# Pacing indirect stores and weight loads, and a re-ordered last stage, in a decoder layer with a mixture of experts

## The reference

```python
def _attn(q_in, k_in, v_in, wq, bq, wk, bk, wv, bv, wo, bo, causal):
    Q = (q_in @ wq + bq).reshape(Bq, Sq, H, HD)      # K, V likewise
    scores = jnp.einsum('bqhd,bkhd->bhqk', Q, Kp) / jnp.sqrt(jnp.float32(HD))
    if causal: scores = jnp.where(mask, scores, -jnp.inf)
    o = jnp.einsum('bhqk,bkhd->bqhd', jax.nn.softmax(scores, axis=-1), V)
    return o.reshape(Bq, Sq, Dm) @ wo + bo

def _moe(x, rw, rb, w1, b1, w2, b2):
    topw, topi = jax.lax.top_k(jax.nn.softmax(xf @ rw + rb, axis=-1), K)
    topw = jax.nn.softmax(topw, axis=-1)
    combine = zeros((T, E)).at[arange(T)[:, None], topi].add(topw)
    h = gelu(einsum('td,edf->etf', xf, w1) + b1[:, None, :])
    eo = einsum('etf,efd->etd', h, w2) + b2[:, None, :]
    return einsum('etd,te->td', eo, combine)

x = _layernorm(x + _attn(x, x, x, ..., True), ln1_g, ln1_b)
x = _layernorm(x + _attn(x, encoder_output, encoder_output, ..., False), ln2_g, ln2_b)
x = _layernorm(x + _moe(x, ...), ln3_g, ln3_b)
```

## Time and profile before

| | before |
|---|---|
| runs | 1040.5, 1038.59, 1041.3 us |
| the profiled execution's own time | 1039.41 us |
| its span (first to last instruction) | 1037.7 us |
| TensorE busy | 977.9 us (94%) |
| ScalarE busy | 585.7 us (56%) |
| VectorE busy | 566.6 us (55%) |
| GpSimd busy | 351.7 us (34%) |
| granted clock of TensorE | 0.9 or more in all slices but three at 0.8 |

### The profile page before, as it was taken

The page is one execution under the profiler, slowest core; times in us unless marked ns, Lnnn a source line. Parts: engine busy times, 40 slices in busy tenths (PEclk is TensorE's granted clock), DMA queues, the critical chain, the costliest instruction groups (busy, mean ns, idle before and its releaser), DMA issues.

```text
span 1037.7 us, 18756 instructions
## 1 busy us (share of the span) xinstructions
PE 977.9 (94%) x6068; PEld 583.6 (56%) x6069; DVE 566.6 (55%) x949; ACT 585.7 (56%) x1201; POOL 351.7 (34%) x481
## 2 busy tenths in 40 slices
PE   5899999999999999999998999988978999999975
PEld 3446444343445543445533354226977999999964
DVE  3646587777767777776777777804221221112127
ACT  2364556777765677765666757865323343443452
POOL 8465962343144443214445042122131111111114
PEclk9999999999999999999999999989998999999988
DMA  7623452003024012108114030022030343333143
GB/s 213 165 79 102 107 135 82 23 19 105 2 69 116 22 42 55 40 1 259 39 48 123 2 92 1 6 83 67 18 108 29 112 132 116 111 106 125 37 127 126
DMA packets 71936, 84.22 MB, mean 81 GB/s; under 512 B 10688, under 2 KB 65472, under 8 KB 71744
## 3 DMA queue, kind: packets, MB, share of 16 engines
q1 hardware_dynamic: 66368, 66.06, 22.2%
q0 software_dynamic: 5504, 17.34, 5.0%
HBM read 38.89 MB, written 12.63 MB: 50 GB/s over the span
## 4 chain that ended last, share of the span: by engine, by line
PE 86%; DMA 3%; SPq 3%; ACT 2%; issue 2%; DVE 2%; POOL 1%; another core or an unknown queue 1%; DVEq 0%; ACTq 0%; POOLq 0%
PE o_bank L798 16%; PE a_bank L781 15%; PE v_slot L1242 11%; PE v_slot L754 11%; PE a_bank L1234 9%; PE a_bank L722 6%; PE a_bank L737 3%; PE o_bank L1234 3%; PE v_slot L758 3%; PE v_slot L820 2%; SPq L498 2%; PE v_slot L806 1%; PE a_bank L702 1%; PE v_slot L759 1%
## 5 line engine op out<-in xcount | busy, mean ns | idle before, releaser
L969 DVE TENSOR_REDUCE max_q<-v_slot 128x1 f32<-128x1024 f32 (+3 forms) x352 | 399.6, 1172 | 115.0 <-PE v_slot L754 72.3
L912 ACT ACTIVATE probs<-a_bank 128x512 f32<-128x512 f32 (+1 forms) x688 | 364.2, 588 | 127.8 <-PE a_bank L781 115.9
L781 PE MATMUL a_bank<-q_stack_cross,k_stack_cross 99*128 99x512 bf16 x512 | 166.0, 386 | 7.3 <-issue 5.4
L1248 ACT ACTIVATE hidden<-a_bank,b 128x128 f32<-128x128 f32 x216 | 79.1, 368 | 163.6 <-PE a_bank L1234 141.5
L754 PE MATMUL v_slot<-k_stack_cross,q_stack_cross 96*128 96x512 bf16 x512 | 148.8, 383 | 2.5 <-DMA k_stack_cross<-parts 2.4
L798 PE MATMUL o_bank<-probs,v_cross 128*32 128x512 f32 x1024 | 133.3, 607 | 0.1
L1242 PE MATMUL v_slot<-stack_or_weights,hidden 128*128 128x256 f32 x576 | 131.0, 381 | 1.1 <-DVEq L1078 1.1
L1234 PE MATMUL a_bank<-x_col,stack_or_weights 128*128 128x128 f32 x864 | 112.6, 282 | 7.2 <-ACT hidden L1248 3.7
L1242 PEld LDWEIGHTS v_slot<-stack_or_weights,hidden 128*128 128x128 f32 x576 | 107.1, 191 | 14.7 <-DVEq L1078 1.3
L1234 PEld LDWEIGHTS a_bank<-x_col,stack_or_weights 128*128 128x128 f32 x864 | 108.5, 198 | 9.7 <-issue 4.1
L781 PEld LDWEIGHTS a_bank<-q_stack_cross,k_stack_cross 99*128 99x128 bf16 x512 | 44.9, 98 | 118.5 <-ACT probs L912 68.8
(11 more groups left out here) (210 smaller groups left out, 1162.0 us busy)
## 6 DMA issues: line engine op xcount, KB each, us to landing
stack_or_weights<-in_e_w SPq DMA_DIRECT2D x16, 1024.0 KB, 6.5
stack_or_weights<-parts SPq DMA_DIRECT2D x96, 128.0 KB, 2.4
k_stack_cross<-parts SPq DMA_DIRECT2D x96, 128.0 KB, 2.5
q_stack_cross<-parts SPq DMA_DIRECT2D x48, 128.0 KB, 2.4
inputs<-in_ctxT POOLq DMA_DIRECT2D x4, 1024.0 KB, 6.7
y_got<-token_out SPq DMA_DIRECT2D x16, 256.0 KB, 6.1
x_slots<-slots_in SPq DMA_DIRECT2D x30, 129.0 KB
inputs<-in_xT POOLq DMA_DIRECT2D x4, 512.0 KB, 6.0
```

What stands on the lines that cost most here:

```text
L781: last = nc.tensor.matmul(bank[:, i * cols:(i + 1) * cols], lhs, q_stack[kind][0:KM, G * u + j, q0:S], start=True, stop=True)
L912: nc.scalar.activation(probs[tile % PB][:, js[0]:js[-1] + 1, q0:S], a_bank[at % AS][:, 0:len(js) * (S - q0)].rearrange("p (j t) -> p j t", ...
L969: nc.vector.tensor_reduce(most, rows, X, ALU.max, negate=True).then_inc(v_free, 1)
L1248: nc.scalar.activation(hidden[:, f, :], h_bank[f % HB][:, 0:P], ACT.Gelu, bias=b1[:, bass.ds(e * FC + f, 1)]).then_inc(flow.gelu_done, 1)
```

## The change

Six things are changed, all in the order of instructions or in the waits ahead of them but the last two.

1. The scatters. Each carries the name of the weighing behind which it stands, and GpSimd waits for that weighing (`pv_done`) before it issues the store.
2. The first two experts' weights. `experts_in` goes; eight halves of matrices (`expert_piece`) stand behind odd weighings that follow the last one of unit 24.
3. The late loads. The fourteen go out in three parts (`LATE`), behind `rows_in` 0, 1 and 2; the bias addition for batch 0 stands behind `rows_in` 3 and no longer behind the maxima of unit 3.
4. Two fills of the cross values' ones and zeros go from GpSimd to VectorE.
5. The softmax over the two chosen experts (class `Weights`) is computed for the twelve row tiles of batches 0 to 2 behind the last score of unit 31, and for the other four in the end; the diagonals of the twelve are made by ScalarE in its loop over experts, three per expert.
6. The last stage. The identity products, now 512 wide, come ahead of the others for all pairs, the last two behind waits for the last tile. VectorE takes mean and gain straight from PSUM in one instruction (`spread_out`), ScalarE multiplies by rstd, GpSimd adds the bias (`move`); for the last two pairs VectorE does both in one instruction.

```diff
-        if ev == ("split", 0, 3):
-            spread.append(("more_loads",))
-        if ev == ("max_parts", 3):
+        if ev[0] == "rows_in" and ev[1] < len(LATE):
+            spread.append(("late_loads", ev[1]))
+        if ev == ("rows_in", len(LATE)):
             spread.append(("add_bias", 0))
         if ev[0] == "place":
-            rows += [("scatter", ev[1] * QT + t, k) for t in range(QT) for k in range(2)]
+            rows += [(ev[1] * QT + t, k) for t in range(QT) for k in range(2)]
         if ev[0] == "weigh" and rows:
-            spread.append(rows.pop(0))
+            spread.append(("scatter", *rows.pop(0), *ev[1:]))
+        if ev == ("weigh", UNIT_NO[B - 1, 0, UNITS - 1], QT - 1):
+            pieces = list(range(PIECES))
+        elif ev[0] == "weigh" and ev[2] % 2 and pieces:
+            spread.append(("expert_piece", pieces.pop(0)))
...
-                elif k == "experts_in":
+                elif k == "expert_piece":
+                    e, piece = divmod(ev[1], PIECES // 2)
+                    matrix, half = divmod(piece, 2)
                     sp.wait_ge(pv_done, NO.last_pv(B - 1, 0, UNITS - 1) + 1)
-                    for i in range(2):
-                        load_weights(sp, i, i)
+                    if matrix == 0:
+                        target, source = w1[e], a["e_w1"][e].rearrange("(c p) n -> p c n", p=P)
+                    else:
+                        target, source = w2[e], a["e_w2"][e].rearrange("(c p) n -> p c n", p=P)
+                    part = slice(half * target.shape[1] // 2, (half + 1) * target.shape[1] // 2)
+                    sp.dma_start(target[:, part, :], source[:, part, :]).then_inc(w_in[e], 16)
...
                 elif k == "scatter":
-                    t, kk = ev[1:]
+                    t, kk, *weighing = ev[1:]
+                    pool.wait_ge(pv_done, NO.pv[tuple(weighing)] + 1)
...
+                elif k == "weights":
+                    first_weights.shift(dve)
+                    first_weights.steps_apart(dve)
+                    first_weights.finish(dve)
...
+            for n in range(6):
+                came_in(n)
+            total = (pe.value_load(first_i[0:1, E - 1:E], min_val=0, max_val=SLOT_TILES) + pe.value_load(tiles_i[0:1, E - 1:E], min_val=1, max_val=TOK // P))
+            pe.wait_ge(main.xcol_ready, total + 1)
+            pe.sem_inc(passed, 1)
+            came_in(6)
+            pe.wait_ge(main.y_evac, total + 1)
+            pe.sem_inc(passed, 1)
+            came_in(7)
             for n in range(TT // FT):
-                pe.wait_ge(mix_ready, 2 * FT * (n + 1))
+                pe.wait_ge(mix_ready, 2 * max(LAST_BATCH, FT * (n + 1)))
                 pe.wait_ge(got[n], 32)
                 for i in range(FT):
                     t = n * FT + i
-                    bank = mix_bank[n][:, i * D:(i + 1) * D]
                     for k in range(2):
-                        nc.tensor.matmul(bank, mix[:, k, t, :], y_got[:, t, k, :], start=(k == 0), stop=False)
-                    last = nc.tensor.matmul(bank, ident[:, :], x2_all[:, t, 0:D], start=False, stop=True)
+                        last = nc.tensor.matmul(mix_bank[n][:, i * D:(i + 1) * D], mix[:, k, t, :], y_got[:, t, k, :], start=False, stop=(i == FT - 1 and k == 1))
                 last.then_inc(mixed, 1)
...
+            def move(n):
+                x2 = x2_all[:, n * FT:(n + 1) * FT, 0:D]
+                pool.wait_ge(scaled_back, FT * (n + 1))
+                nc.gpsimd.tensor_tensor(x2, x2, ln_gb[:, 5:6, :].to_broadcast([P, FT, D]), ALU.add).then_inc(moved, 1)
...
+                for i in range(FT):
+                    t = n * FT + i
-                    nc.scalar.activation(x2_all[:, t, 0:D], mix_bank[n][:, i * D:(i + 1) * D], ACT.Identity, bias=shift_m[:, t:t + 1],
-                                         scale=fin_rstd[:, t:t + 1]).then_inc(normed, 1)
+                    nc.scalar.activation(x2_all[:, t, 0:D], x2_all[:, t, 0:D], ACT.Identity, scale=fin_rstd[:, t:t + 1]).then_inc(scaled_back, 1)
...
+            def spread_out(n):
+                for t in range(n * FT, (n + 1) * FT):
+                    last = nc.vector.scalar_tensor_tensor(x2_all[:, t, 0:D], mix_bank[n][:, (t % FT) * D:(t % FT + 1) * D], fin_mv[:, t, 0:1], ln_gb[:, 4, :],
+                                                          ALU.subtract, ALU.mult)
+                last.then_inc(stretched, 1)
...
-                nc.vector.tensor_tensor(x2, x2, bet, ALU.add).then_inc(fin_ready, 1)
+            for n in ON_VECTOR:
+                dve.wait_ge(root_ready, n + 1)
+                dve.wait_ge(stretched, n + 1)
+                for t in range(n * FT, (n + 1) * FT):
+                    last = nc.vector.scalar_tensor_tensor(x2_all[:, t, 0:D], x2_all[:, t, 0:D], fin_rstd[:, t:t + 1], ln_gb[:, 5, :], ALU.mult, ALU.add)
+                last.then_inc(fin_ready, 1)
```

More of the change, by code:

```diff
@@ L45 @@
 EARLY_LEAST = 2
+PIECES = 8
 CHOICE, PLACING = 2 * QT + 4, 9
@@ L150, in in_order @@
             n, kt = ev[1:]
-            if n == UNIT_NO[B - 1, 0, UNITS - 1] and kt == QT - 1:
-                order.append(("experts_in",))
             if kt == key_tiles(UNIT_LIST[n][1]) - 1:
@@ L462, in decoder_layer @@
+        WEIGHT_STEPS = 6
+        first_weights, last_weights = Weights(0, LAST_BATCH, 0, 0), Weights(LAST_BATCH, TT, 1, WEIGHT_STEPS)
+        FIRST_PIECES = 16 * PIECES // 2
         CASTS = 8
@@ L1311, in count_tiles @@
             nc.vector.tensor_copy(first_i[:, :], first_f[:, :]).then_inc(counts_ready, 1)
[L1313 to L1314 removed]
+            last_weights.shift(dve)
         block = ctx.enter_context(nc.Block())
```

180 lines of the change are left out of this document (103 added, 77 removed).

## The result

| | before | after |
|---|---|---|
| median of five runs | 1040.77 us | 1028.68 us |
| lowest to highest | 1038.59 to 1041.3 | 1027.64 to 1033.36 |
| ratio, 95% interval | | 0.9895 [0.9878, 0.9912] |
| span of the profiled execution | 1037.7 us | 1025.9 us |

The change takes 12.1 us off by the medians and 10.9 by the ratio; I had forecast 5.5. The direction and the range were right, the size about half of what was measured. The profiled executions differ by 11.8 us, and where these lie can be read by following one landmark after another through both traces.

The account below looks back on a forecast made before the run. TensorE, holding 86% of the chain of waits, was taken as the bound. Terms -2.4 - 2.4 - 3.1 + 8.4 + 2.0 - 7.6 = -5.1 us took 1039.4 to 1034.3, forecast as 1035, range 1027 to 1043.

Parts of the forecast that it names:

- step 1: Start: late loads in three parts let the first maxima leave early, ending TensorE's 2.44 us wait; -2.4 us.
- Step 2: Near 490 us: expert weights in eight pieces end TensorE's 2.38 us wait for the splits' copies; -2.4 us.
- 3 batch 1: Scatters of batch 1, each behind a weighing, about 3 us apart: most of the burst's 3.9 us returns; -3.1 us.
- Step 4: Scatters of batch 2 paced: two thirds of 6.0 us lost return; weighing (31, 1) ends at 691.2, not 695.2.
- Step 5: First second products wait for last batch 2 scatter, ten serial tile loads, bias load; +8.4 us with step 4 inside.
- step 6: Behind TensorE's 13 us stand before the first second products, a low clock costs +2.0 us, bounds 1 and 3.
- Step 9: Last stage: earlier identity products, pairs at 2.3 us on GpSimd; VectorE ends at 1025.7, not 1033.34; -7.6 us.
- The rival in which the bias chain doesn't bite: First second products not held by the bias load, the norm sets their start; -18.8 us, 1020.6; chance 0.08.
- The rule: Last stage: VectorE with at most one SBUF input doesn't contend with GpSimd; GpSimd 2.1 us a pair, end 1.4 sooner.
- Step 7: Early weights of twelve tiles delay o_bank's last evacuation some 0.7 us, hidden by the wait of step 5.

Follow-up runs that it names:

- b2_between: Changed kernel with the expert-bias load b2 moved between the tile loads of the first and second early expert, not behind all ten; 1014.28 us, ratio 0.9757.
- b2_ungate2: b2_between without the wait for weighings at the eight scatters of batch 2; 1020.78 us, ratio 0.981.
- ungate2: Changed kernel without the wait for weighings at the eight scatters of batch 2 alone; 1022.31 us, ratio 0.9835.
- pieces_back: Changed kernel with all eight halves of the first two experts' matrices issued at once, where the four whole ones stood before; 1032.59 us, ratio 0.9935.
- tail_only: Changed kernel with late loads, expert weights and scatters as before, leaving last stage, early weights, diagonals and fills; 1030.2 us, ratio 0.993.
- late_back: Changed kernel with all fourteen late loads ahead of the first maxima again, and batch 0's bias addition moved back with them; 1030.02 us, ratio 0.991.
- ungate_all: Changed kernel without any wait for weighings at the scatters of batches 0 to 2; 1026.01 us, ratio 0.9869.
- pads_after: b2_between with SyncE waiting for the last batch's eight stores before it issues the eight pad stores; 1015.06 us, ratio 0.9778.
- rank_spaced: b2_between with GpSimd fills between the last batch's eight stores, so about 2.2 us apart and not 1.27; 1014.18 us, ratio 0.975.
- rank_interleaved: rank_spaced with the store of the early tile's rows put between the third and fourth of the eight stores; 1005.52 us, ratio 0.9677.

## Why the prediction was right in sign and too small in size

The terms beside what the two traces show, in us:

| step | predicted | traces |
|---|---|---|
| 1 late loads (with the fills moved) | -2.4 | -2.9 |
| 2 expert weights | -2.4 | -4.1, and 1.6 of the clock at 520 to 530 |
| 3 batch 1 | -3.1 | -3.8 |
| 4 batch 2, to the end of weighing (31, 1) | -4.0 | -7.0 |
| 5 from there to the second products | +12.4 (35.9 for 23.5) | +13.0 (36.5 for 23.5) |
| 6 clock behind the stand | +2.0 | +1.5 (5.21 for 3.72) |
| 9 last stage | -7.6 | -6.8 (34.2 for 40.9) |
| sum | -5.1 | -11.7 |

- **Step 5** was the decision of the forecast and held: ten serial loads from 680.25 us, TensorE standing 13.89 us (13 forecast), the low clock behind it. Its size held with some luck: from the last store's issue to the first tile load it took 4.2 us, not 2.5, and the bias load 5.0 us to TensorE's start, not 6.7. b2_between removed this chain and gained 14.4 us; the table has 14.5 for steps 5 and 6, b2_between's own trace 13.8, so the close match is in part chance. b2_ungate2 and ungate2 show both sides of the wait. The rival in which the bias chain doesn't bite (1020.6, given 0.08) is the case of b2_between, which came out 6.3 us lower still.
- **Step 4** is the term that failed most. The prediction said "the first five scatters are still only 1.75 us apart, so I take two thirds of that back". They stood 1.4 to 1.75 us apart, and the stall was nevertheless gone whole; ungate2 and b2_ungate2 bring it back whole. I had 6.0 us as the whole loss; it was 7.0 between the two traces.
- **Step 2** was sized by the idle time alone, -2.4 us. The prediction's own step 6 counted a clock behind a wait, but here I left it out, though the stretch of before at 490 to 500 us shows it: 2.38 us of wait and 1.7 of clock are the 4.1. pieces_back took 4.2 us more than the changed kernel by the ratios and 5.1 by the spans, 1.6 of these by the chance near 520 us.
- **Steps 1 and 3** were right within 0.7 us. For step 1 tail_only, which has the late loads as before, waits 1.75 us and not 2.44: a part of the gain at the start comes with the other edits there or with chance (its trace is 2.2 us ahead of before from 120 us on), and late_back's timing can't tell 1.5 from 2.9. So the 2.9 of the table isn't the late loads' own.
- **Step 9**: the size held within 0.9 us. I had GpSimd as the bound at 2.3 us a pair; a pair takes 1.98. Its own instructions need 1.90; VectorE has no gap either, but 0.17 us of its 1.98 pass in an instruction that ends with GpSimd's addition. Which of the two sets the pace no run separates: VectorE alone would come to 1.81 a pair, GpSimd to 1.90 and a gap, so GpSimd as the bound is the likelier, and only its price was too high. A two-statistics step takes 0.75, two spread_out 0.85 (0.78 forecast). The 0.9 us are lost behind VectorE's end: it ends 7.7 us closer to the last expert tile, but 5.3 us ahead of the end of the span, not 4.4.
- **The rule.** The power takes 0.69 to 0.72 us in all eight pairs, never 1.19, and the addition beside spread_out takes 1.18 or 1.19, near the mean of 1.16 of the same shape in L605. The Trainium skill, "SBUF — State Buffer", Who interferes with whom, says that only the port pair that VectorE and GpSimd share makes one wait for the other; spread_out reads one of its tensors from PSUM. The trace agrees, and the step of 2.1 us that I gave as that rule's result was nearer than the 2.3 that I took. But the rule as the prediction puts it, that a VectorE instruction with at most one SBUF input does not contend, fails for the addition of epsilon, which reads one SBUF tensor and was held from 0.17 to 0.34 us. There the page excepts VectorE's two-port modes, which I had left out; whether this instruction ran in one, no row shows.
- **Step 7** is hidden in the changed kernel by the wait of step 5, as said. Without that wait it shows, but small: in b2_between the turn of the last o_bank waits 1.03 us for ScalarE, for 0.87 in before, 0.2 and not 0.7.

What stays open is what holds the engines during a burst of indirect stores. The trace of before names no instruction as releaser; a DMA view of 755 to 764 us, most of ScalarE's stand of 8.40 us, has only these two queues:

```profile
q0 software_dynamic: 333, 0.91, 28.4%
q1 hardware_dynamic: 496, 0.46, 15.2%
```

The whole trace has two more queues, of the kind `instruction`, and none of their packets falls into this stall, nor into that of batch 1 (before, ungate_all) or of the last batch in b2_between and pads_after; in the stall of batch 2 there are one or two. So loading of instructions isn't seen to be the cause. The DMA engines are 44% busy on average, which speaks against their bandwidth, though single slices of 0.2 us reach 90%. Which of the eight stores starts the stall, and how far apart they must be, was not tried: eight at 1.27 us stall, eight at 2.2 do not, nor do the first five of batch 2 in after at 1.4 to 1.75. The last four of batch 0, some 1.3 us apart in every trace (504.70 to 508.58 us in after), leave TensorE without a gap, so the spacing alone isn't enough either; but it had a projection of 3.6 us to work on then.

## What to carry to other kernels

Before a wait is added to an instruction, list what is queued behind it on its engine and on the engines that wait for it: here one load at the end of such a queue turned 5.5 us of gain into 6.2 of loss, and moving it was worth more than the whole change. Price a stall as its idle time and the low clock behind it, read from the same trace, not the idle time alone (2.38 and 1.7 us for the expert weights). If a fix shows no gain in the time, look in the trace whether its stall is gone and a new wait stands behind it: rank_spaced and rank_interleaved differ by the place of one store and by 7.6 us.

## What the runs showed of the hardware that was not expected

- During eight indirect stores 1.27 us apart ScalarE, VectorE and TensorE stand at once; the idle times marked for it are 1.9 to 9.6 us, ordinary waiting included. 2.2 us apart they do not. Taking the pad stores from beside them changed nothing (TensorE's wait 5.24 and 5.36 us).
- Between 519 and 532 us TensorE ran at half clock for some 3.4 us, with no idle time, in seven of the fourteen executions profiled, and at full clock in the other seven; two executions of the same instructions differ. In all seven it starts 0.7 to 1.6 us behind the end of the router's sixteen products of 8 columns, which the other seven have as well. Each time it costs 1.7 us, so a difference of that size between two profiles can be this alone.
- A VectorE instruction on 128x2 numbers (L1587) takes 0.17 us beside an idle GpSimd and 0.32 to 0.35 us beside GpSimd's addition, ending 0.01 to 0.03 us behind it, in six pairs of all eleven traces with the new last stage. A saturated pair of engines can each look like the bound.
- Where the main loop starts, TensorE waits 2.36 us and then 1.52 to 1.80 us, and runs at half clock for 4 to 5 us behind that, in every version; nothing here touched it.
